# Layer 0's query, key and value projections: from f32 matmuls per tile to three fp32r products, queries and keys for two tiles at once

## The reference, cut to what matters

```python
qkv = x @ W_qkv                              # 256 -> 768, float32
q, k, v = jnp.split(qkv, 3, axis=2)          # 16 heads of 16
ret = einsum('bhtd,bhsd->bhts', q, k) * decay
r = einsum('bhts,bhsd->bhtd', ret, v) + einsum('bhtd,hde->bhte', q, past_kv) * 256
y = r.transpose(0, 1, 3, 2)
yn = (y - mean(y)) * rsqrt(var(y) + eps) * gn_weight + gn_bias     # one mean and variance per batch
x = layernorm(x + yn)
```

## Time and profile before

| | |
|---|---|
| median of 3 runs | 901.35 us (900.93 to 901.55) |
| the profiled execution's own time | 900.24 us |
| its span, first to last instruction | 898.6 us |
| busy: TensorE, VectorE, ScalarE, GpSimd | 822.4, 601.6, 484.7, 269.1 us |
| mean granted TensorE clock | 0.971 |
| layer 0 in the span | from 7.3 us to about 225 us |

### The profile page before, as it was taken

How to read it: one execution, slowest core, us unless ns; L and a number is a source line. 1 busy time by engine, 2 the same in 40 slices (tenths; PEclk the granted TensorE clock), 3 DMA queues, 4 the chain that set the end, 5 groups by cost and what they waited for, 6 DMA issues and landing times. The chain is left out here.

```text
span 898.6 us, 23310 instructions
## 1 busy us (share of the span) xinstructions
PE 822.4 (92%) x8906; PEld 670.6 (75%) x8906; DVE 601.6 (67%) x1403; ACT 484.7 (54%) x1008; POOL 269.1 (30%) x333
## 2 busy tenths in 40 slices
PE   6999999999899999998999899998899779999960
PEld 5888888887577777766777688886555549999950
DVE  3677778777557777777655335676667876757627
ACT  2544444443777777766964245654664315455425
POOL 1266663221202222223000000224452042656344
PEclk9999999999999999999999999999999789999985
DMA  8500000000000000002477444443222213566439
GB/s 320 193 25 18 18 23 18 20 9 3 1 1 1 1 2 1 1 1 71 125 195 182 108 128 116 127 147 135 95 94 94 94 36 112 140 193 166 122 63 341
DMA packets 74637, 79.55 MB, mean 89 GB/s; under 512 B 21824, under 2 KB 65728, under 8 KB 74176
## 3 DMA queue, kind: packets, MB, share of 16 engines
q1 hardware_dynamic: 69584, 72.36, 26.2%
q0 software_dynamic: 3968, 5.25, 3.4%
q10 hardware_dynamic: 1008, 0.91, 0.3%
HBM read 50.70 MB, written 27.79 MB: 87 GB/s over the span
## 5 line engine op out<-in xcount | busy, mean ns | idle before, releaser
L727 DVE TENSOR_TENSOR r_prob<-r_pS,const 128x512 f32<-128x512 f32 x128 | 81.9, 681 | 24.7 <-PE r_pS L549 24.7
L1104 DVE SCALAR_TENSOR_TENSOR f_gl<-att_res,small_first,f_gh 128x512 fp32r<-128x512 f32 x64 | 47.3, 747 | 35.8 <-ACT f_gh L1029 33.5
L958 PE MATMUL f_pY<-wpjT,f_gh 128*128 128x256 f32 x256 | 65.4, 290 | 0.3 <-DVE f_gl L1104 0.3
L1671 POOL TENSOR_TENSOR att_res<-att_res,t_hy 128x1024 f32<-128x1024 f32 x8 | 15.5, 1960 | 165.0 <-DVEq L2141 165.0
L959 PE MATMUL f_pY<-wpjT,f_gl 128*128 128x256 f32 x256 | 62.7, 279 | 0.0
L1372 PEld LDWEIGHTS q_bank<-q_xT,att_res 128*64 128x64 f32 x1024 | 57.3, 140 | 7.2 <-issue 4.2
L2507 POOL DMA_INDIRECT sum_dram<-e_yo,y_id x24 | 43.1, 1795 | 60.1 <-ACT e_yo L2641 45.0
L1372 PE MATMUL q_bank<-q_xT,att_res 128*64 128x128 f32 x1024 | 60.9, 279 | 0.0
L958 PEld LDWEIGHTS f_pY<-wpjT,f_gh 128*128 128x128 f32 x256 | 48.1, 188 | 15.9 <-issue 13.4
L1023 ACT ACTIVATE att_res<-f_pH 128x512 f32<-128x512 f32 x64 | 38.0, 594 | 38.6 <-PE f_pH L943 37.8
L2622 ACT ACTIVATE e_hh<-e_pH 128x320 fp32r<-128x320 f32 x64 | 26.2, 433 | 53.7 <-PE e_pH L2546 53.4
(11 more groups left out here) (321 smaller groups left out, 2354.5 us busy)
## 6 DMA issues: line engine op xcount, KB each, us to landing
kv_dram<-att_res SPq DMA_DIRECT2D x32, 256.0 KB, 3.4
t_ring<-kv_dram SPq DMA_DIRECT2D x128, 64.0 KB, 2.3
wi<-L_ffn_wi SPq DMA_DIRECT2D x8, 1024.0 KB, 5.0
wo<-L_ffn_wo SPq DMA_DIRECT2D x8, 1024.0 KB, 7.8
x_res<-L_attn_x SPq DMA_DIRECT2D x8, 512.0 KB, 6.9
q_dram<-att_res SPq DMA_DIRECT2D x16, 256.0 KB, 3.4
t_q<-q_dram SPq DMA_DIRECT2D x8, 512.0 KB, 4.1
x_dram<-x_res SPq DMA_DIRECT2D x8, 512.0 KB, 3.0
```

The source lines that it names most:

```text
L727: dve.tensor_tensor(prob[t % 2][:, r, :, :], pS[r][:, :, :], dec[:, r, :, :], ALU.mult)\
L958: pe.matmul(out, gh[c % 4][:, cols], net.wpjT[:, c, :], start=(c == 0 and t % 2 == 0), stop=False, skip_group_check=True)
L1104: dve.scalar_tensor_tensor(out=gl[c % 4][:, :], in0=g[c][:, :], scalar=net.lnw[:, c:c + 1], in1=gh[c % 4][:, :], op0=ALU.mult, op1=ALU.sub ...
```

## The change

Each product of x and W becomes a sum of three products of type fp32r: the high parts xh and wh (a copy into the fp32r type), the low parts xl = x - xh and wl = w - wh, and the terms wh xh + wh xl + wl xh. Only the first pair of tiles keeps the plain f32 product. Queries and keys are made for two tiles at a time, 256 columns per matmul, in a bank `pQK` that they use in turn; values are still made tile by tile, in a bank `pVK` whose other half now takes the turned keys. Keys of the pair (2, 3) are made in step 0, its queries in step 1, those of the next batch's pair (0, 1) in steps 2 and 3. ScalarE makes wh once and xh of each pair (`high_x`) and takes queries for two tiles at once; GpSimd makes xl (`low_x`), but VectorE makes wl and the first xl. x is loaded tile by tile into a buffer per pair; of the first loads on ScalarE's queue, that of tile 1 moves ahead of the small weights, and the first product waits for both of its tiles. The core of the diff:

```diff
-    pQV = ps("pQV", [P, 512])
-    pQ, pV = pQV[:, 0:DIM].rearrange("p (k t) -> p k t", k=KD), pQV[:, DIM:2 * DIM]
-    pKK = ps("pKK", [P, 512])
-    pKT, pK = pKK[:, 0:DIM].rearrange("p (k t) -> p k t", k=KD), pKK[:, DIM:2 * DIM]
+    pQK = ps("pQK", [P, KD, 2, P])
+    pVK = ps("pVK", [P, 512])
+    pV, pK = pVK[:, 0:DIM], pVK[:, DIM:2 * DIM]
...
     def gpsimd(pool):
+        def low_x(b, j):
+            if isinstance(b, int) and b == 1 and j == 0:
+                pool.wait_ge(qk_made.sem, qk_made.after(3))
+            pool.wait_ge(high_ready.sem, high_ready.after(2 * b + j + 1))
+            pool.tensor_tensor(xl[j][:, :, :], xT[j][:, :, :], xh[j][:, :, :], ALU.subtract).then_inc(x_split.sem, 1)
...
             for t in range(TPB):
+                if t % 2 and behind:
+                    low_x(b + 1, t // 2)
                 decay_queries(b, t)
...
     def scalar(act):
+        def take_queries(b, j):
+            act.wait_ge(qk_made.sem, qk_made.after(2 * (2 * b + j) + 2))
+            act.wait_ge(r_made.sem, r_made.after(b * TPB + 2 * j + 2 - TPB))
+            nc.scalar.activation(qT2[j][:, :, :, :].rearrange("p t k n -> p k t n"), pQK[:, :, :, :], ACT.Copy)
+            for odd, mask in enumerate(("even", "odd")):
+                ins = nc.scalar.activation(qEO2[j][:, :, :, odd, :].rearrange("p t k n -> p k t n"), pQK[:, :, :, :], ACT.Copy, scale=net.table[mask])
+            ins.then_inc(q_copied.sem, 1)
+
+        def high_x(b, j):
+            act.wait_ge(x_in[j].sem, x_in[j].after(32 * (b + 1)))
+            if not isinstance(b, int) or b:
+                act.wait_ge(v_made.sem, v_made.after((b - 1) * TPB + 2 * j + 2))
+            nc.scalar.activation(xh[j][:, :, :], xT[j][:, :, :], ACT.Copy).then_inc(high_ready.sem, 1)
...
             for t in range(TPB):
+                if t % 2 and behind:
+                    high_x(b + 1, t // 2)
                 if t + 1 < TPB:
                     take(b, t + 1)
                 elif behind:
                     take(b + 1, 0)
+                if t == 1:
+                    take_queries(b, 1)
+                elif t == 3 and behind:
+                    take_queries(b + 1, 0)
...
-        act.dma_start(xT[0][:, :, :], a["xT"][0]).then_inc(x_in[0].sem, 16)
+        act.dma_start(half_of(0), a["xT"][0]).then_inc(x_in[0].sem, 16)
+        act.dma_start(half_of(1), a["xT"][1]).then_inc(x_in[0].sem, 16)
         act.dma_start(net.small0[:, :], a["small0"]).then_inc(small0_in.sem, 16)
-        act.dma_start(xT[1][:, :, :], a["xT"][1]).then_inc(x_in[1].sem, 16)
...
+        nc.scalar.activation(wh[:, :, :], w[:, :, :], ACT.Copy).then_inc(high_ready.sem, 1)
+        high_x(0, 1)
+        take_queries(0, 0)
         take(0, 0)
...
     def tensor(pe):
+        def project(b, j, at, bank):
+            if isinstance(b, int) and 2 * b + j == 0:
+                pe.wait_ge(x_in[0].sem, x_in[0].after(32))
+                terms = [(w, xT[0])]
+            else:
+                terms = [(wh, xh[j]), (wh, xl[j]), (wl, xh[j])]
+            terms = [(ws, xs, k) for ws, xs in terms for k in range(KD)]
+            for m in range(KD):
+                for n, (ws, xs, k) in enumerate(terms):
+                    mm = pe.matmul(bank[:, m, :, :], ws[:, k, at + m * P:at + (m + 1) * P], xs[:, k, :].rearrange("p (t n) -> p t n", t=2),
+                                   start=(n == 0), stop=(n == len(terms) - 1))
+            mm.then_inc(qk_made.sem, 1)
+
+        def keys_of(b, j):
+            q = 2 * b + j
+            pe.wait_ge(x_split.sem, x_split.after(q))
+            pe.wait_ge(q_copied.sem, q_copied.after(q))
+            project(b, j, DIM, pQK)
+
+        def queries_of(b, j):
+            pe.wait_ge(k_taken.sem, k_taken.after(2 * b + j + 1))
+            project(b, j, 0, pQK)
+
+        def values_of(b, t):
+            i, j = b * TPB + t, t // 2
+            if not isinstance(b, int) or i:
+                pe.wait_ge(v_taken.sem, v_taken.after(i))
                 turned = b * (TPB - 1) + max(t - 1, 0)
                 if not isinstance(turned, int) or turned:
                     pe.wait_ge(ks_ready.sem, ks_ready.after(turned))
...
+            for n, (ws, xs, k) in enumerate(terms):
+                mm = pe.matmul(pV, xs[:, k, mine], ws[:, k, 2 * DIM:], start=(n == 0), stop=(n == len(terms) - 1))
+            mm.then_inc(v_made.sem, 1)
...
         def batch(b, before, behind):
             for t in range(TPB):
                 if t + 1 < TPB:
-                    project(b, t + 1)
+                    values_of(b, t + 1)
                 elif behind:
-                    project(b + 1, 0)
+                    values_of(b + 1, 0)
+                if t < 2 or behind:
+                    (keys_of, queries_of)[t % 2](*((b, 1) if t < 2 else (b + 1, 0)))
...
     def vector(dve):
+        def take(b, j, bank=None):
+            dve.wait_ge(qk_made.sem, qk_made.after(2 * (2 * b + j) + 1))
+            dve.tensor_copy(kT2[j][:, :, :, :].rearrange("p t k n -> p k t n"), pQK[:, :, :, :] if bank is None else bank).then_inc(k_taken.sem, 1)
...
-                if t + 1 < TPB:
-                    take(b, t + 1)
-                elif behind:
+                if t == 0:
+                    take(b, 1)
+                elif t == 2 and behind:
                     take(b + 1, 0)
```

More of the change, by code:

```diff
@@ L285, in retention @@
     small_in, small0_in, later_in = sig("small_in"), sig("small0_in"), sig("later_in")
-    x_in, x_full = [sig(f"x_in{t}") for t in range(TPB)], sig("x_full")
+    x_in, x_full = [sig(f"x_in{j}") for j in two], sig("x_full")
+    high_ready, x_split = sig("high_ready"), sig("x_split")
     fc_in, pj_in = sig("fc_in"), sig("pj_in")
@@ L387, in gpsimd @@
         for t in range(TPB):
+            if t % 2:
+                low_x(1, t // 2)
             decay_queries(0, t)
@@ L397, in gpsimd, with batch @@
         pool.wait_ge(steps.sem, steps.done(1))
-        def batch(b):
+        def batch(b, behind=True):
             for t in range(TPB):
+                if t % 2 and behind:
+                    low_x(b + 1, t // 2)
                 decay_queries(b, t)
@@ L409, in gpsimd @@
             batch(b)
-        with pool.Fori(5, BATCH) as b:
+        with pool.Fori(5, BATCH - 1) as b:
             steps.enter(b - 5, 5)
             batch(b)
-            steps.leave(BATCH - 5)
+            steps.leave(BATCH - 6)
+        batch(BATCH - 1, False)
         group_pow(BATCH - 1)
@@ L511, in tensor @@
         pe.wait_ge(w_in.sem, w_in.after(16))
[L513 to L519, removed]
-                for k in range(KD):
-                    pe.matmul(pQ[:, m, :], w[:, k, m * P:(m + 1) * P], xT[t][:, k, :],
-                              start=(k == 0), stop=(k == KD - 1))
-            for k in range(KD):
-                mm = pe.matmul(pV, xT[t][:, k, :], w[:, k, 2 * DIM:], start=(k == 0), stop=(k == KD - 1))
-            mm.then_inc(qv_made.sem, 1)
-            if not first:
-                pe.wait_ge(k_taken.sem, k_taken.after(i))
+        def project(b, j, at, bank):
+            if isinstance(b, int) and 2 * b + j == 0:
+                pe.wait_ge(x_in[0].sem, x_in[0].after(32))
+                terms = [(w, xT[0])]
+            else:
+                terms = [(wh, xh[j]), (wh, xl[j]), (wl, xh[j])]
[15 more added lines that the diff above has]
+            i, j = b * TPB + t, t // 2
+            mine = slice(t % 2 * P, (t % 2 + 1) * P)
+            if not isinstance(b, int) or i:
+                pe.wait_ge(v_taken.sem, v_taken.after(i))
                 turned = b * (TPB - 1) + max(t - 1, 0)
@@ L531, in project @@
                     pe.wait_ge(ks_ready.sem, ks_ready.after(turned))
-            for m in range(2):
-                for k in range(KD):
-                    mm = pe.matmul(pKT[:, m, :], w[:, k, DIM + m * P:DIM + (m + 1) * P], xT[t][:, k, :],
-                                   start=(k == 0), stop=(k == KD - 1))
-            mm.then_inc(kT_made.sem, 1)
+            if isinstance(b, int) and 2 * b + j == 0:
+                terms = [(w, xT[0])]
+            else:
+                terms = [(wh, xh[j]), (wh, xl[j]), (wl, xh[j])]
+            terms = [(ws, xs, k) for ws, xs in terms for k in range(KD)]
+            for n, (ws, xs, k) in enumerate(terms):
+                mm = pe.matmul(pV, xs[:, k, mine], ws[:, k, 2 * DIM:], start=(n == 0), stop=(n == len(terms) - 1))
+            mm.then_inc(v_made.sem, 1)
         def scores(b, t, before):
             i = b * TPB + t
-            pe.wait_ge(qv_taken.sem, qv_taken.after(i + 1))
-            pe.wait_ge(k_taken.sem, k_taken.after(i + 1))
+            pe.wait_ge(q_copied.sem, q_copied.after(2 * b + t // 2 + 1))
+            pe.wait_ge(k_taken.sem, k_taken.after(2 * b + t // 2 + 1))
             pe.wait_ge(s_taken.sem, s_taken.after(4 * i))
@@ L548, in scores @@
                     rows = slice(32 * r, 32 * r + 32)
```

(5 more changed lines are left out.)

64 lines of the change are left out of this document (39 added, 25 removed).

## The result

The changed kernel takes **932.5 us** (median of 4 runs, 932.2 to 936.8), the kernel before 901.1 beside it (898.96 to 901.55, 4 runs): a ratio of 1.035, 95% interval 1.032 to 1.038. The forecast was 922 with a range of 909 to 930. So the direction was right, and the time lies 2.5 us above the range.

The account below looks back on a forecast made before the run. Layer 0 was taken as bound by TensorE, with VectorE right behind. The profiled 900.24 + 11.4 (wait) + 8.3 (start) + 1.0 (clock) = 920.9, median 922 us; own range 916 to 928, wider range 909 to 930.

Parts of the forecast that it names:

- TensorE's own work: Layer 0 projections: fp32r matmuls 0.12 us apart, 4.2 us per pair against 5.3, 16 us of TensorE work gone.
- The moved wait: Values, first in TensorE's step, now wait for the decayed keys: batch 28.55 us, +11.4 us over six periods.
- The clock: At the start, about 4 us of TensorE idling may halve its rate: 0 to +2.3 us, taken as +1.
- the page's rule: Trainium skill: TensorE's clock falls to half in idle gaps of a kernel fed too late; used for the start's upper end.
- The start: ScalarE splits tiles 2 and 3 before taking first queries; scores of tile 1 at 29.0 us instead of 20.68: +8.3.
- The covers: In layer 0, other work hides ScalarE's query copies and `high_x` and GpSimd's `low_x`; otherwise TensorE waits by their lateness.
- TensorE alone: Rival: TensorE sets layer 0's pace and the new wait costs nothing; 15.4 us less, 9.3 more at start: 895; chance 0.10.
- The loads of tiles 2 and 3: Rival at the start: these loads land early, start costs 4 instead of 9: 918; within likeliest case, no separate chance.

Follow-up runs that it names:

- The filled pause: Changed kernel plus eight unused bf16 matmuls in step t=1 of batches 1 to 7, ahead of the wait on the decayed keys: 927.2 us.
- the early loads: Changed kernel with the first x loads of tiles 1, 2 and 3 issued on SyncE's queue instead of ScalarE's: 925.7 us.
- the last kernel: Changed kernel with keys/queries before values, early x loads, second pair's split moved, ten warming products, batch 1's x earlier, batch 0's split later: 899.0 us against 902.9.
- the run with keys and queries first: Changed kernel with two calls swapped, so each TensorE step forms keys or queries before the values that wait for decayed keys: 907.2 us.

## Why the prediction was right and wrong

- **TensorE's own work: right.** Two fp32r matmuls of 256 columns every 0.24 us, as forecast. Small miss: the first two behind a wait take 0.34, so a step's projections are 2.26 us and not 2.10.
- **The moved wait: right in kind and nearly in size.** Forecast "some 30 us over seven batches", measured 28.8. Steps at full clock: 7.44 for tile 1 to 2 (forecast 7.23), 6.82 for 2 to 3 (6.62), 14.6 for 3 to 1 (14.7). The 0.2 us too little in each of the first two is mostly the 0.16 above: 2.4 us over six periods.
- **The clock: the step that failed.** The forecast priced the half clock at one pause, the start ("I take +1"), in the same text that built a pause of 3 us into every batch, and put the clock behind those pauses at nothing without a reason. It fell behind that pause in four of the six periods, whose steps from tile 3 to 1 are 16.11, 16.07, 15.88 and 16.38, against 14.63 and 14.57: 1.5 us each, 6 us. With it 920.9 becomes 927, and the 2.4 above make it 929.3; the start, batch 0 and what lies behind (1.3, 1.0 and 1.0) fill the rest up to the profiled 932.66. The filled pause shows that this is the clock: with it the batches are 28.8 us long. A smaller pause was not free either: behind the 1.39 us in batch 7 half clock came too, and the two steps there take 14.1 us, against 12.4 with the early loads, where it did not come. The forecast applied the page's rule only to the start, where a row of its own showed an idle engine.
- **The start: near in size by luck, wrong in mechanism.** +10.6 against +9.3. The split's load did land at 17.36 (forecast 17.5), but the split did not hold the first queries: ScalarE waited another 0.62 us for them. They were late because the first product waited for the x of tile 1 till 12.41, 5.1 us later than before, and then ran at half rate; the forecast took it to be done by 16 to 17 and did not price that wait. The values of tile 1 then waited 0.72 us and not 4, and ran at the full rate (1.13 us for four), so the half clock was not where the +1 stood:

```profile
21.03 1.13 PE L604 MATMUL r_pVK<-w_first,r_xT 128*128 128x256 f32 x4 [0.72 <-ACT r_v L456]
```

  It came one step later, behind the pause of 2.01 us ahead of the values of tile 2. The scores of tile 0 start at 23.52 (forecast 22.9), those of tile 1 7.80 us behind them (6.1). The +1.0 of batch 0 is spread over its three steps, some 0.3 us each, where the forecast had +0.2 in all and took nothing.
- **The covers held.** ScalarE's and GpSimd's new work in the loop stayed hidden, but GpSimd's subtract is 1.3 us, above the 0.73 and under the 1.46 of the bounds, and its collision with the state update costs 0.4 us a batch once the wait is gone. In the changed kernel the update of 1.66 us (98.26 to 99.92) is still done before `carry_in` needs it at 100.06.
- **The rivals.** TensorE alone (895) was wrong for a reason beyond the wait: even with the wait gone, the saved matmuls are worth 0.1 to 0.2 us a batch in the loop, since VectorE's chain and ScalarE's results stand right behind TensorE. Full TensorE in the earlier trace rows said who was last, and not by how much. The loads of tiles 2 and 3 did not land early (17.36), and the sum of that rival, 922 less 5, is 917 and not 918.

## What to carry to other kernels

When a bank is shared in a new way, look at which instruction in the step carries its wait: the same wait cost 0.3 us at the end of the step and 3 us at its head, and two swapped calls were worth 25 us. Whoever writes a new pause into a sum should give it, in the same line, the price of half clock behind it, or the reason why there is none. And taking work from an engine that is full is worth only the distance to the engine behind it: compute that distance first.

## What the runs showed of the hardware

- The clock fell behind some pauses in TensorE's records and not behind others, and their length alone does not say which. In the changed kernel pauses of 2.01 (ahead of 27.04), 2.56, 2.56, 2.57, 3.14 and even 1.39 us (ahead of 241.38) were followed by half clock, those of 2.59 and 2.57 us (83.36 and 203.37) were not. A pause of 1.57 us in batch 7 was followed by it in the last kernel (209.53), and not in the run with keys and queries first (218.52). The half clock of 113.0 lasted some 3 us.
- The first products after the idle start run at half rate (3.75 us against 1.9 for eight records) while their windows show a granted clock of 1.00. Ten bf16 products ahead of them bring the full rate (1.05 us against 2.04 in the kernel before).
- One subtract of 128x512 on GpSimd between SBUF operands made two state updates on VectorE take 1.66 us (98.26 in the changed kernel) instead of 0.61, and left VectorE's products out of PSUM at 0.63 us each.
- One kernel's runs spread with its mean granted clock: of 27 runs of the kernel before the shortest had 897.4 us at 0.977, the longest 905.3 at 0.968. Differences of 2 us could be told only with a dozen runs a side, if at all.
